# Bias of the attention gate: from a product on TensorE to an addition on VectorE

## The reference

```python
def _L1_xattn_ref(query, kv, Wq, Wg, bg, Wkv, Wo):
    q = query @ Wq.T
    gate = jax.nn.sigmoid(query @ Wg.T + bg)
    ...
    kv_summary = jnp.einsum('bhsd,bhse->bhde', k, v)
    z = 1.0 / (jnp.einsum('bhld,bhd->bhl', q, k_sum)[..., None] + EPS)
    attn = jnp.einsum('bhld,bhde->bhle', q, kv_summary) * z
    out = attn * gate @ Wo.T
    return out
```

## Time and profile before

| | |
|---|---|
| median of 3 runs | 1104.53 us (1104.44 to 1106.37) |
| the profiled execution | 1107.26 us, span 1105.5 us |
| TensorE products, busy | 1048.1 us, 95% of the span |
| VectorE busy | 673.4 us, 61% |
| ScalarE busy | 591.9 us, 54% |
| POOL busy | 281.9 us, 26% |
| mean granted clock of TensorE | 0.986 of full speed |

### The profile page before, as it was taken

One profiled execution on the slowest core, in us unless ns is written; L12 is line 12 of the kernel. 1 busy time (PEld: TensorE's weight loads), 2 busy tenths in 40 slices (PEclk: granted clock), 3 DMA queues, 4 the chain that ended last, 5 costly groups with the idle time before them and its releaser, 6 DMA issues.

```text
span 1105.5 us, 16228 instructions
## 1 busy us (share of the span) xinstructions
PE 1048.1 (95%) x5830; PEld 824.7 (75%) x5830; DVE 673.4 (61%) x1226; ACT 591.9 (54%) x890; POOL 281.9 (26%) x445
## 2 busy tenths in 40 slices
PE   7999999979999999989999999899899999999994
PEld 5887777766455555568888888688687899999993
DVE  6746555435998998665655655466823666666660
ACT  5765787734898898853333244121113466666651
POOL 1012222113555553100000034100010044444442
PEclk9999999989999999999999999999999999999998
DMA  6682666521100000201111232302043588888853
GB/s 213 227 303 97 172 173 188 163 68 59 30 20 20 30 20 11 97 1 68 48 58 51 101 108 77 100 29 77 1 152 111 181 236 223 225 227 230 231 132 39
DMA packets 47606, 127.03 MB, mean 115 GB/s; under 512 B 5810, under 2 KB 6834, under 8 KB 46772
## 3 DMA queue, kind: packets, MB, share of 16 engines
q1 hardware_dynamic: 36516, 97.53, 26.1%
q0 software_dynamic: 10448, 27.58, 11.0%
q10 hardware_dynamic: 576, 1.05, 0.3%
HBM read 97.76 MB, written 28.38 MB: 114 GB/s over the span
## 4 chain that ended last, share of the span: by engine, by line
PE 67%; DVE 5%; ACT 3%; issue 2%; POOL 1%; DMA 0%; ACTq 0%; DVEq 0%; POOLq 0%
PE bank L54 16%; PE bank L55 15%; PE bank L56 15%; PE bank L1819 9%; PE bank L1840 4%; PE bank L3812 1%; PE bank L1831 1%; DVE s_hot_tile L3975 1%; PE bank L1913 1%; PE bank L1895 1%; DVE s_pick L3972 1%; PE bank L1924 1%; PE bank L1849 1%; PE bank L1923 1%; DVE s_mid L3999 0%
## 5 line engine op out<-in xcount | busy, mean ns | idle before, releaser
L1819 PE MATMUL bank<-w,f_qT 128*128 128x512 bf16 x512 | 117.9, 379 | 0.2 <-DVE f_h L2060 0.2
L3651 POOL DMA_INDIRECT out<-e_y,scatter_idx x32 | 69.0, 2157 | 115.7 <-ACT e_y L3746 111.5
L1819 PEld LDWEIGHTS bank<-w,f_qT 128*128 128x128 bf16 x512 | 48.7, 98 | 50.8 <-issue 0.6
L3688 ACT ACTIVATE s_m_h<-s_mid 128x512 fp32r<-128x512 f32 (+1 forms) x24 | 15.1, 631 | 126.9 <-DVE s_mid L3999 76.3
L3639 POOL DMA_INDIRECT e_xg<-xn_rows,gather_idx x32 | 33.7, 1054 | 172.6 <-DVE gather_idx L3989 105.7
L54 PE MATMUL bank<-wkv_h,ctx_h_all 128*128 128x512 f32 x128 | 54.0, 422 | 12.0 <-DVE wkv_l L708 7.4
L1840 PE MATMUL bank<-w,f_q2T 128*128 128x512 bf16 x256 | 59.5, 387 | 2.4 <-ACT f_q2T L1593 2.4
L54 PE MATMUL bank<-e_xT_h,e_wg_h 128*128 128x256 f32 (+1 forms) x192 | 56.5, 294 | 2.9 <-issue 2.1
L2060 DVE SCALAR_TENSOR_TENSOR f_h<-bank,f_columns,f_sg 128x512 f32<-128x512 f32 x64 | 47.9, 749 | 13.8 <-ACT f_sg L1577 6.8
L4077 DVE TENSOR_TENSOR e_mid<-bank,e_sil 128x256 f32<-128x256 f32 (+1 forms) x48 | 20.3, 423 | 55.5 <-ACT e_sil L3720 55.4
L55 PE MATMUL bank<-e_xT_l,e_wu_h 128*128 128x256 f32 (+1 forms) x192 | 54.1, 282 | 0.0
(11 more groups left out here) (415 smaller groups left out, 3289.9 us busy)
## 6 DMA issues: line engine op xcount, KB each, us to landing
wraw<-in_wffn SPq DMA_DIRECT2D x48, 512.0 KB, 4.2
e_raw_g<-in_ew_gate SPq DMA_DIRECT2D x16, 704.0 KB, 4.0
e_raw_u<-in_ew_up SPq DMA_DIRECT2D x16, 704.0 KB, 5.4
e_raw_d<-in_ew_down SPq DMA_DIRECT2D x16, 512.0 KB, 6.5
sorted_y<-e_y SPq DMA_DIRECT2D x19, 256.0 KB, 4.3
x_rows<-rows SPq DMA_DIRECT2D x16, 256.0 KB, 2.0
xn_rows<-a_work SPq DMA_DIRECT2D x16, 256.0 KB, 2.0
s_raw<-x_rows SPq DMA_DIRECT2D x16, 256.0 KB, 2.7
```

The lines of the kernel that those rows point to most:

```text
L1819: ins = pe.matmul(bank[c % 2][:, :], qT[t % 2][:, k * P:(k + 1) * P], w_gv(k, col + c * 512), start=(k == 0), stop=(k == KD - 1))
L3651: gp.indirect_dma_start(io["out"], bass.IndirectOffsetOnAxis(g.scatter_idx[:, slot:slot + 1], 0), e_y[t][u][:, :], None, compute_op=ALU.ad ...
L3688: ins = act.activation(m[0][r, c, :], mid[n % 2][r, :], ACT.Copy)
```

## The change

SP loads the bias into all 128 partitions of `bg` (now plain fp32) by one broadcast, once tile 14 has been turned. POOL's memset, ScalarE's `bias()` and VectorE's subtraction are gone, with the entry `"bg"` in the order of weights. `gate(s)` ends with its twelfth product. A new function `add_bias(s)` on VectorE adds the bank and `bg` into `th`; ScalarE's `tanh(s)` works on `th` in place. TensorE waits for the addition (`gated`) before it reuses the bank, where it waited for the tanh. In VectorE's list `add_bias(0)` stands before the loop and `add_bias(s+1)` behind `a_normalise(s-1)` in front of `a_split_x(s-2)`.

```diff
--- before.py
+++ after.py
@@ -1311,9 +1311,8 @@
         work = Cursor(nc, wide_q).take("a1_work", [P, 4 * D], fp32)
         att = [work[:, u * D:(u + 1) * D] for u in range(2)]
         a_xn = [work[:, (2 + u) * D:(3 + u) * D] for u in range(2)]
-        bg_raw = att[1]
         after_xn = Cursor(nc, turned_rows)
-        bg, th = after_xn.take("a1_bg", [P, D], f32r), after_xn.take("a1_th", [P, D], fp32)
+        bg, th = after_xn.take("a1_bg", [P, D], fp32), after_xn.take("a1_th", [P, D], fp32)
         after_w3 = Cursor(nc, g.w3_at)
         wq, wg, wo = [[after_w3.take(f"a1_{n}_{part}", [P, KD, D], f32r) for part in "hl"] for n in ("wq", "wg", "wo")]
         raw = raw_q, raw_g, raw_o
@@ -1360,8 +1359,8 @@
 
         w_in = [sem(f"{n}_in") for n in ("wq", "wg", "wo")]
         w_hi, w_lo = sem("w_hi"), sem("w_lo")
-        bg_in, zeroed, r_in = [sem(n) for n in "bg_in zeroed r_in".split()]
-        FIRST = {0: 0, 1: KD, "bg": 2 * KD, 2: 2 * KD + 1, "r": 3 * KD + 1}
+        bg_in, gated, r_in = [sem(n) for n in "bg_in gated r_in".split()]
+        FIRST = {0: 0, 1: KD, 2: 2 * KD, "r": 3 * KD}
         summ_in = sem("summ_in")
         gate_ready, th_ready, n_ready, dz_ready, z_ready, nz_ready = [sem(n) for n in "gate_ready th_ready n_ready dz_ready z_ready nz_ready".split()]
         att_ready, aT_ready, aT_hi, aT_lo = [sem(n) for n in "att_ready aT_ready aT_hi aT_lo".split()]
@@ -1421,9 +1420,8 @@
                 sp.wait_ge(q2_low, TT)
                 sp.wait_ge(q2_high, TT)
                 weights(2, io["wo"])
-                sp.wait_ge(q2T_ready, 2 * TT)
-                for row in (0, HD):
-                    sp.dma_start(bg_raw[row:row + 1, :], io["bg"]).then_inc(bg_in, 16)
+                sp.wait_ge(xT_ready, TT - 1)
+                sp.dma_start(bg[:, :], io["bg"][0, :].partition_broadcast(P)).then_inc(bg_in, 16)
                 for s in range(TT):
                     if s in (2, 6, 10):
                         sp.wait_ge(n_ready, s + 2)
@@ -1518,9 +1516,6 @@
                     if have(i + 2):
                         scales(i + 2)
                         largest(i + 2)
-                    if i == TT + 1:
-                        gp.wait_ge(xT_ready, TT - 1)
-                        gp.memset(f(bg[:, :]), 0.0).then_inc(zeroed, 1)
                     if have(i - 2):
                         after(i - 2)
                     if have(i + 2):
@@ -1632,10 +1627,8 @@
                     act.activation(a_q[b % 2][0][:, c * S:(c + 1) * S], e[n % 2][:, :], ACT.Copy).then_inc(feature_hi, 1)
 
                 def tanh(s):
-                    act.wait_ge(gate_ready, s + 1)
-                    if s:
-                        act.wait_ge(att_ready, s)
-                    act.activation(th[:, :], a_gbank[:, :], ACT.Tanh, scale=0.5).then_inc(th_ready, 1)
+                    act.wait_ge(gated, s + 1)
+                    act.activation(th[:, :], th[:, :], ACT.Tanh, scale=0.5).then_inc(th_ready, 1)
 
                 def split_att(s):
                     act.wait_ge(aT_ready, s + 1)
@@ -1656,13 +1649,6 @@
                 def query(n):
                     phi(n)
                     split_q(n)
-
-                def bias():
-                    act.wait_ge(zeroed, 1)
-                    act.wait_ge(bg_in, 32)
-                    for row in (0, HD):
-                        ins = act.activation(bg[row:row + 1, :], bg_raw[row:row + 1, :], ACT.Copy)
-                    ins.then_inc(w_hi, 1)
 
                 act.wait_ge(ones_ready, 1)
                 context(0)
@@ -1715,7 +1701,6 @@
                 split_q(1)
                 for k in range(KD):
                     split_w(1, k)
-                bias()
                 normalise(TT - 1)
                 query(2)
                 split_x(TT - 1)
@@ -1864,16 +1849,14 @@
 
                 def gate(s):
                     if s:
-                        pe.wait_ge(th_ready, s)
+                        pe.wait_ge(gated, s)
                     else:
                         pe.wait_ge(feature_ready, CT + 2)
                     for k in range(KD):
                         if s == 0:
                             pe.wait_ge(w_lo, FIRST[1] + k + 1)
-                        mm3(pe, a_gbank[:, :], [x[:, k, tokens(s)] for x in (g.xT_h, g.xT_l)], [x[:, k, :] for x in wg], k == 0, False)
-                    if s == 0:
-                        pe.wait_ge(w_lo, FIRST["bg"] + 1)
-                    pe.matmul(a_gbank[:, :], g.ones_r[:, :], bg[:, :], start=False, stop=True).then_inc(gate_ready, 1)
+                        last = mm3(pe, a_gbank[:, :], [x[:, k, tokens(s)] for x in (g.xT_h, g.xT_l)], [x[:, k, :] for x in wg], k == 0, k == KD - 1)
+                    last.then_inc(gate_ready, 1)
 
                 def attend(s):
                     b, t = s // 4, s % 4
@@ -1970,7 +1953,7 @@
                         route(s - 3)
                 turn_att(TT - 1)
                 pe.wait_ge(nz_ready, 2 * TT)
-                pe.wait_ge(th_ready, TT)
+                pe.wait_ge(gated, TT)
                 pe.wait_ge(feature_ready, CT + TT)
                 shared["expand"](0, 0)
                 project(TT - 1)
@@ -2137,6 +2120,15 @@
                     v.wait_ge(th_ready, s + 1)
                     v.scalar_tensor_tensor(out=mine[:, :], in0=th[:, :], scalar=1.0, in1=mine[:, :],
                                            op0=ALU.add, op1=ALU.mult).then_inc(att_ready, 1)
+
+                def add_bias(s):
+                    v.wait_ge(gate_ready, s + 1)
+                    if s == 0:
+                        v.wait_ge(bg_in, 16)
+                        v.wait_ge(xT_ready, TT)
+                    else:
+                        v.wait_ge(att_ready, s)
+                    v.tensor_tensor(th[:, :], a_gbank[:, :], bg[:, :], ALU.add).then_inc(gated, 1)
 
                 def split_att(s):
                     v.wait_ge(aT_hi, s + 1)
@@ -2214,8 +2206,6 @@
                 split_q(1)
                 for k in range(KD):
                     split_w(1, k)
-                v.wait_ge(w_hi, FIRST["bg"] + 1)
-                v.tensor_tensor(bg[HD:HD + 1, :], bg_raw[HD:HD + 1, :], f(bg[HD:HD + 1, :]), ALU.subtract).then_inc(w_lo, 1)
                 residual(TT - 1)
                 query(2)
                 split_x(TT - 1)
@@ -2224,6 +2214,7 @@
                     split_w(2, k)
                 v.wait_ge(w_hi, FIRST["r"] + 1)
                 v.tensor_tensor(r_hl[:, :, E1:2 * E1], r_raw[:, :, :], f(r_hl[:, :, 0:E1]), ALU.subtract).then_inc(w_lo, 1)
+                add_bias(0)
                 for s in range(TT):
                     if s:
                         split_att(s - 1)
@@ -2234,6 +2225,8 @@
                     if s:
                         a_statistics(s - 1)
                         a_normalise(s - 1)
+                    if s + 1 < TT:
+                        add_bias(s + 1)
                     if s >= 2:
                         a_split_x(s - 2)
                 split_att(TT - 1)
```

## The result

Before, the median of 22 executions is 1106.43 us (1103.42 to 1112.02); changed, it is 1109.49 us. The ratio is 1.0027 with an interval of 1.0015 to 1.0038, so 3.1 us slower by the medians. The changed kernel was measured again in two later sessions: 1109.19 (1.0011, 0.9994 to 1.0028) and 1108.48 (1.0020, 1.0005 to 1.0035). (Two of the 22 executions of the changed kernel, at 1178 and 1179 us and a mean clock of 0.843, are left out of the ratio; without them the median is 1109.38.) The profiled execution took 1108.13 us.

What follows compares the result with a forecast made beforehand. TensorE was taken to bound steps 0 to 11, ScalarE and VectorE the entry, a longer chain the last four steps. 0.94 + 2.56 - 1.5 = 2.0 us less, from 1104.53 to 1102.5 us, range 1100.4 to 1104.4.

Steps and rivals of the forecast that it cites:

- Entry: Before the loop: without the bias preparation `residual(15)` and `attend(0)` start 0.94 us earlier; bounds 0 to 0.94.
- the bias product of `gate(0)`: At the entry: removing it gives nothing, since TensorE waits 2.7 us behind it anyway.
- The load: Bias broadcast on SP's queue: issued 20 us before it is wanted, costs nothing; without that cover 3.1 us.
- `add_bias(0)`: VectorE's add before `a_weigh(0)`: 0.69 us, hidden, costs nothing; with no cover 0.69.
- Query steps: Steps 0 to 10: eleven bias products of 0.233 us gone, 2.56 us saved; longer chain hidden with 1.8 us to spare.
- Last steps: Last four steps, without `query`: the chain with add and tanh is uncovered; loss 1.38 us, taken as 1.5.
- the one on the clock: TensorE's waits before `attend(0)` and in the last steps: one more clock fall would leave 0.3 us less; outside the sum.
- the price of 1.7 us a fall: From `contract(15)`: its 16 products take 5.30 us at the lower clock in place of 3.61.
- sign of being wrong: One of several signs that would show the forecast wrong: a granted clock below 1 between 484 and 655 us.
- the "slower" rival: Clock falls at `attend(0)` and the last four `project`s, 1.7 us each; two give 1105.9, three 1107.6; 5%.

Runs made afterwards that it cites:

- fill_one: The changed kernel with one unread TensorE product added behind `gate(0)`; 1109.90 us, its profiled execution 1102.84 us.
- late: The changed kernel with the add moved to the head of `a_weigh`, behind `split_att`, and tanh behind ScalarE's `split_att`; 1104.82 us, 0.9977 of before.
- fill_entry: The changed kernel with 11 unread products in TensorE's wait before `attend(0)`; 1105.48 us, where the changed kernel had 1109.19.
- fill_tail: The changed kernel with four unread products in front of each of the last four `project`s; 1109.31 us, ratio 1.0023 to before.
- before_early: The kernel before with VectorE's bias subtraction moved behind `residual(15)`; 1107.13 us, ratio 1.0000.

## Why the prediction was wrong

Forecast were 1102.5 us (1100.4 to 1104.4) and no or a small gain; measured were 1109.49. 1.9 of the 7.0 us are the base: the median of three executions was low. The other 5.1 are the change: 3.1 slower where 2.0 faster was forecast.

- Entry: 0.94 forecast, 0.95 in the profile, 0.93 in fill_one. Right. That the bias product of `gate(0)` gives nothing: right.
- The load and `add_bias(0)`: nothing forecast. The latter is hidden: S0 comes 15.10 us behind `attend(0)` without a fall, 15.32 before; the difference is the product of gate 1.
- Query steps: 2.56 forecast for eleven products; 2.40 in the ten from S0 to S10 and 0.22 in the first, 2.62. Right, and the chain stayed hidden with the starts worked out.
- Last steps: a loss of 1.38 by the chain that the prediction builds, taken as 1.5; 49.22 - 47.86 = 1.36 measured without a fall; cycles of 9.24 and 10.28 against 9.25 and 10.29. Right.
- The sum of these is 2.0 forecast, 2.2 in fill_one. The mechanism of the work and its sizes hold.
- The step that failed is the one on the clock. The prediction saw the risk and kept it out of the sum, at 5% for two or more falls, with the reason that the waits of the last steps "stay under the 2.05 that cost the clock here". A fall came after 1.38 us there, in late after 0.7. For `attend(0)`, where most was lost, it had no such reason, only that the clock read 1.00 behind 2.7 us in one profile. And the price of 1.7 us a fall was that of `contract(15)`; at `attend(0)` it was 3.0 (18.07 - 15.10; 2.8 in the two later profiles), since the clock stayed low for twice as long. With 3.0 there, 1.5 in the last steps and 1.0 behind, 5.5 us of falls stand against 2.2 of work, which is the 3.3 us from C to the end. The prediction's own sign of being wrong, a granted clock below 1 between 484 and 655, came. This is the "slower" rival, by its mechanism and two of its five places.
- A fall in `contract(15)` in the one profile I had was read as the price that any further fall would have. Before pays nothing for it, nor for the one at `gate(0)`. Before's falls lie under cover, those of the changed kernel on the path; that asymmetry was missed.
- The 1.0 after the last steps: from S15 to the end the three profiles of the changed kernel take 442.7 to 442.9 us, the three of before 441.7 to 442.1. In each of the former the clock's loss near 800 us is twice that of before, 3.4 against 1.7. fill_entry and fill_tail, whose work is the same there, lose 1.7 and take 442.0 and 441.7. So this too goes with the clock; why it stays low for twice as long there no experiment tested. Windows 798 to 808, before and changed:

```profile
798.00:808.00 10.00, 7.12 (x35) 5.88 (x36) 7.10 (x18) 3.07 (x5) 0.00 (x0) 0.83 0.00 0
```

```profile
798.00:808.00 10.00, 7.39 (x33) 6.30 (x34) 6.82 (x18) 3.07 (x5) 0.12 (x1) 0.66 0.00 0
```

## What to carry to other kernels

A wait of TensorE has two prices: its length, and the clock of the products behind it. So a change that takes a few tenths of work from TensorE and puts a hop between engines in front of its next product can lose more by the clock than it wins, and the sum must have a term for it: for each wait that grows, what follows it, and whether that is the path. Unread products in the one long wait on the path, and the new instruction placed behind the chain instead of in it, turned 3 us slower into 5.5 us faster.

## What the runs showed of the hardware

- Falls come in fixed amounts. Every stretch with a lower granted clock outside the last 20 us loses 1.7 us of full speed or 3.4, in all profiles; the clock is at half in it.
- Between 460 and 660 us they follow waits of 2.9, 2.5, 2.05 and 1.4 us, in fill_entry one of 0.85 and in late one of 0.7, and not every such wait: the 2.7 in front of `attend(0)` had none in the profiles of before, before_early and fill_one, nor did 3.3 us near 700 us in fill_one and fill_both. The Trainium skill, TensorE: Matmul & The Clock Gate, Part 1, names a longer idle time than these, up to 2.9 us, as what throttles TensorE; here shorter waits did, and the measurement decides. Why one such wait is followed by a fall and another is not stays open.
- The 35 executions of before in the first session spread by 9 us (1103.3 to 1112.3), with the mean granted clock between 0.980 and 0.989. Their standard deviation is 2.5 us; with the clock's loss taken off each it is 1.1. So much of what looks like noise is the clock.
